# Attention and mixture-of-experts kernel: the maxima's split and the routing steps of five portions moved in the order of the work

## The reference

```python
# attention: 16 heads of 8, causal, keys and values from ctx (120 positions)
h = layernorm(x)
Q, K, V = h @ wq.T + bq, ctx @ wk.T + bk, ctx @ wv.T + bv
p = softmax(where(causal & not padded, Q K^T / sqrt(8), -inf))
x = x + (p V) @ wo.T + bo
# experts: 8, each token goes to its best 2; one shared expert for all
h = layernorm(x)
s = sigmoid(h @ gate_w + bias); top, idx = top_k(s, 2); w = top / (sum(top) + 1e-6)
o = 0.1 * (shared_mlp(h) + sum_k w_k * mlp[idx_k](h))       # mlp: 128 -> 512 -> gelu -> 128
x = x + o / (max|o| + 1e-6)
```

## Time and profile before

| | |
|---|---|
| profiled execution | 850.22 us, span 848.50 us |
| PE busy | 755.0 us (89%) |
| VectorE (DVE) busy | 646.8 us (76%) |
| ScalarE (ACT) busy | 636.9 us (75%) |
| GpSimd (POOL) busy | 539.9 us (64%) |
| mean granted TensorE clock | 0.968 |

### The profile page before, as it was taken

How to read it: one execution, slowest core, us unless ns; L and a number is a source line. 1 busy time by engine, 2 the same in 40 slices (tenths; PEclk the granted TensorE clock), 3 DMA queues, 4 the chain that set the end, 5 groups by cost and what they waited for, 6 DMA issues and landing times.

```text
span 848.5 us, 21662 instructions
## 1 busy us (share of the span) xinstructions
PE 755.0 (89%) x6977; PEld 512.5 (60%) x6977; DVE 646.8 (76%) x1774; ACT 636.9 (75%) x1185; POOL 539.9 (64%) x634
## 2 busy tenths in 40 slices
PE   5899899987998999988978869999999999979994
PEld 2345455544554555444445647788888888868773
DVE  5766778789688786876756796877778787767897
ACT  3589889877777787777579958888888888869630
POOL 6566666879777887777567773156656665654540
PEclk9999999999999999999898989999999999999998
DMA  4552544441222122211101144667767788782973
GB/s 127 178 192 63 187 137 125 139 146 58 75 66 74 58 86 66 75 60 58 36 8 48 60 160 145 227 236 262 259 236 248 273 296 278 269 279 88 276 232 100
DMA packets 100934, 126.97 MB, mean 150 GB/s; under 512 B 20919, under 2 KB 82039, under 8 KB 94807
## 3 DMA queue, kind: packets, MB, share of 16 engines
q1 hardware_dynamic: 92183, 107.08, 39.4%
q0 software_dynamic: 8640, 18.50, 6.2%
HBM read 77.84 MB, written 39.64 MB: 138 GB/s over the span
## 4 chain that ended last, share of the span: by engine, by line
PE 52%; POOL 13%; DVE 12%; issue 11%; ACT 9%; SPq 2%; DMA 1%; DVEq 0%; ACTq 0%; POOLq 0%
PE bank L1373 5%; PE bank L1385 4%; PE bank L1459 4%; PE bank L1460 4%; PE bank L1461 4%; PE bank L1448 4%; PE bank L1449 4%; PE bank L1450 4%; POOL xs_scratch L1227 4%; ACT prob L781 4%; POOL y_scratch L1234 3%; POOL prob L1212 3%; PE bank L1369 2%; PE bank L1353 2%; PE bank L1328 2%
## 5 line engine op out<-in xcount | busy, mean ns | idle before, releaser
L781 ACT ACTIVATE prob<-bank,padb,sc 120x512 f32<-120x512 f32 x256 | 178.1, 776 | 71.5 <-PE bank L1373 71.4
L1234 POOL DMA_INDIRECT y_scratch<-yo,ti x142 | 141.3, 995 | 121.3 <-DVE yo L1135 89.4
L1212 POOL TENSOR_SCALAR_AFFINE_SELECT prob<-prob 120x512 f32<-120x512 f32 x256 | 159.6, 634 | 81.4 <-ACT prob L781 76.1
L853 DVE TENSOR_REDUCE nm<-bank 128x4 f32<-128x480 f32 x256 | 150.3, 649 | 54.6 <-PE bank L1353 54.5
L1112 DVE TENSOR_TENSOR gl<-gf,gh 128x512 fp32r<-128x512 f32 (+1 forms) x220 | 143.2, 655 | 47.0 <-ACT gh L829 46.0
L1227 POOL DMA_INDIRECT xs_scratch<-x2r,idx x128 | 129.4, 1011 | 33.4 <-issue 32.7
L829 ACT ACTIVATE gh<-gf 128x512 fp32r<-128x512 f32 (+1 forms) x220 | 132.5, 602 | 5.1
L823 ACT ACTIVATE gf<-bank,wt 128x512 f32<-128x512 f32 (+1 forms) x156 | 99.8, 640 | 5.2 <-DVE gl L1112 4.7
L1373 PE MATMUL bank<-qblk,kT 32*120 32x512 f32 x512 | 74.8, 628 | 0.0
L1385 PE MATMUL bank<-prob,vm 120*32 120x128 f32 x2048 | 70.7, 280 | 2.7 <-ACT vm L750 1.6
L1353 PE MATMUL bank<-kblk,qT 32*128 32x480 f32 x512 | 71.9, 633 | 1.0 <-DMA kblk<-kT 1.0
(11 more groups left out here) (202 smaller groups left out, 1660.7 us busy)
## 6 DMA issues: line engine op xcount, KB each, us to landing
wt<-w_scratch SPq DMA_DIRECT2D x39, 1032.0 KB, 5.1
xt<-xs_scratch SPq DMA_DIRECT2D x32, 280.0 KB, 4.7
w_scratch<-x2t SPq DMA_DIRECT2D x8, 1024.0 KB
wt<-y_scratch SPq DMA_DIRECT2D x28, 256.0 KB, 4.9
xs_scratch<-padc SPq DMA_DIRECT2D x15, 280.0 KB, 2.8
x<-in_x SPq DMA_DIRECT2D x16, 256.0 KB, 3.2
qblk<-qT SPq DMA_DIRECT2D x64, 64.0 KB
x_scratch<-x SPq DMA_DIRECT2D x16, 256.0 KB, 2.4
```

What stands on the lines that cost most here:

```text
L781: e.activation(prob[u % NP][0:LK, :], banks[bi][0:LK, :], ACT.Exp, scale=sc[0:LK, 0:1], bias=padb[0:LK, t:t + 1]).then_inc(a_ex, 1)
L853: e.tensor_reduce(nm[:, g, i // 2, :], bk[:, 0:480].rearrange("p (j k) -> p j k", j=4), AX.X, ALU.max, negate=True).then_inc(v_mx, 1)
L1212: e.affine_select(out=pv, in_=pv, compare_op=ALU.is_ge, fill=0.0, base=0, pattern=[[0, 4], [1, 128]], channel_multiplier=-1).then_inc(p_cu ...
L1234: e.indirect_dma_start(y_dram, bass.IndirectOffsetOnAxis(ap=ti_[r % NWS][:, c:c + 1], axis=0), yo_[r % NYO][:, c, :], None).then_inc(d_y[r ...
```

## The change

It moves stages in the order. No instruction is added or removed.

```diff
         if n < NG - 1:
-            at(o + 3 + .43, "nm", n)
+            at(o + 3 + .20, "nm", n)
             at(o + 3 + .84, "nmT", n)
...
     for p, (a, z) in enumerate(PORTIONS):
         s = 7.0 * (4 * z + 10) - end
-        times = LATE_PORTION.get(p, (s + .8, s + 4.8, s + 11.8, s + 32.6, s + 32.8, s + 25.8, s + 38.9, 7.0))
+        times = LATE_PORTION.get(p, (s + .8, s + 25.8, s + 39.8, s + 47.0, s + 53.0, s + 53.4, s + 58.9, 7.0))
         for (stage, i), time in zip((("er", 0), ("route", 0), ("route", 1), ("rank", 0), ("place", 0), ("route", 2)), times):
```

## The result

Six runs of the changed kernel took 856.50 to 865.38 us, median 861.03; six of the kernel before, taken with them, had a median of 850.89. The ratio is 1.0116 (95% interval 1.0074 to 1.0158): the change makes the kernel slower, where 839 us was predicted. The profiled execution took 862.87 us, its span 861.1 (before 848.50); PE is busy 756.0 us, about as before (755.0).

A forecast was written before the change was run, and what follows sets the result against it. The first phase was taken as bound by a TensorE-ScalarE loop with 25.8 us of stalls. Terms summed to -12.2 us, 850.22 to 838.0 profiled, predicted median 839.0 us; range 833 to 845, over cases 829 to 849.

The forecast's parts named there:

- rank to kind 0, place to the next slot: First phase: rank keeps one of two banks, k waits for oT and tz starts 1.9 us later, five times; costs 9.5 us.
- nm behind the maxima: Six slots with scatters: nm no longer stands behind nb2, so nmT follows tO at once; gains 15.1 us.
- The portions' moves without the hold: Route 0's and the weights' collision gain of 10.7 us, less 1.5, 1.0 and 1.0 us for split, route 0, router.
- Route 0: Moved to kind 1, it frees its place in kind 2 and just fits the new one; costs 0.2 us five times.
- nmT's wait below 6 us: Sign of being right: nmT's wait for nm on TensorE falls from 18.8 us to under 6.
- PEld's wait for oT at k in exactly five slots: Sign of being right: k waits for oT in exactly five slots of kind 1, these some 2 us longer.
- place and route 2 ahead of router: In kind 1 on VectorE, router stands behind both and V waits for its bank; costs 0.2 us five times, 1.0 us.
- slots of kind 3 below 8 us: Sign of being right: no slot of kind 3 takes above 8 us with scatters running.
- 315 us for the twelve groups: Sign of being right: the twelve four-slot groups of the first phase take about 315 us instead of 326.62.
- rival 3: GpSimd's selects hold nm's second instruction at its new place, norm to oT wait; 20 us in five groups, 859 us; 9%.
- Rival 4: nm comes early, but nmTs, behind nb2 and route 1, is late for B; half of 15.1 us returns, 846.5 us; 6%.
- Rival 2, the clock: The bank's wait drops TensorE's clock, 1.7 us five times, 8.5 us more, 847.5 us; 17%.

The follow-up runs named there:

- run 9: Changed kernel with place directly behind rank, so rank's bank goes back at once but behind x2T's; ratio 1.0038 to the kernel before.
- run 10: As run 9, with rank and place together moved ahead of x2T, so PV gets a long-free bank; ratio 0.9822 to the kernel before.
- run 5: Changed kernel with rank behind PV and tO of the same slot, so only k and tz share a bank; 850.62 us.
- run 1: Changed kernel without the hold: rank directly in front of place, its bank given back at once; 839.67 us.
- run 2: Kernel before with only nm moved behind the last maxima; 841.15 us, ratio 0.9870.
- run 7: Run 1 with route 1 one slot on, in kind 0, where VectorE waits for a load anyway; 837.41 us.
- run 8: Run 7 with portion 5's route 0 also one slot on; 833.42 us, ratio 0.9791 to the kernel before.
- run 3: Changed kernel with nm back at its old place, so only the portions' steps and scatters are moved; 860.51 us.
- run 11: Run 1 with nm back at its old place, so neither nm's move nor the hold; 847.85 us, ratio 0.9944.

## Why the prediction was wrong

**The step that failed is "rank to kind 0, place to the next slot".** It said that with one bank "k waits for oT", tz for kT, 1.9 us five times. I listed PV among the stages that must take the other bank, and then priced only k and tz. PV comes first, and the other bank is the one that x2T has just filled, behind four exps on ScalarE. The changed kernel shows both, the PV hop 2.19 us and the tz hop 0.75. In the twelve groups PV's hop alone is worth 16.9 us (run 9 against 10), k's and tz's alone 9.1 (run 5 against 1), together 334.96 - 315.49 = 19.5. They don't add: where PV is late, ScalarE has emptied everything else, oT follows PV at once, and the k stretch is only 7.22 us against 6.71 where the clock is whole. It is whole in two of the five. In the others TensorE runs at 1.2 GHz for 3.4, 3.4 and 6.8 us from about PV's wait on, and the k stretches take 8.74, 7.75 and 9.10 us: 3.9 of the 19.5. The step held 9.5 us; 10.0 are missing.

**The terms of the gain were too large.** Without the bank the prediction has -22.3 us for the twelve groups (-15.1 - 10.7 + 1.5 + 1.0 + 1.0); run 1 has 315.49 - 326.62 = -11.1.

- "nm behind the maxima" at -15.1: alone it brings 317.26 - 326.62 = -9.4 (run 2). The wait goes, and the five slots priced at 11.6 give 12.6. But the sixth, priced at 3.5, gets 0.9 longer, since nmTs is late there (run 2), and the one at 173.00 grows by 1.6: I gave the neighbours nothing back.
- The portions' moves without the hold at -7.2: measured 315.49 - 317.26 = -1.8. Route 0 itself came out about as said: the two stretches at its old place take 359.14 - 346.15 = 12.99 us in the changed kernel (13.61 in run 1) where they took 8.72 + 6.34 (from 338.43, around), and the one at its new place is no longer than before, 6.64 us. But route 1, to which the prediction gives no cost, since it stays in a slot of kind 3, came to stand beside selects. That costs three stretches 0.9 us each, 2.7 of the missing 5.4 (run 7, 3.0 by run 8); the rest stays open.

These two, 11.2 us, the bank's 10.0, a start 1.1 us later and an end 2.5 us longer than priced make 24.8 of the 24.9 us between 838.0 and 862.87. The end, 861.1 - 437.95 = 423.15 us against 420.02, lay anywhere from 418.3 to 422.8 in runs 1, 3, 5, 7 and 8, which keep the scatters' move, so I can't say what of it is the late scatters.

**What was right.** Of the signs named: nmT's wait below 6 us, rs2 directly behind the selects, B not stopped beside route 0, PEld's wait for oT at k in exactly five slots, V not late. place and route 2 ahead of router show no cost: the stretch with V is 5.20 us, in the kernel before 5.19. Not so: slots of kind 3 below 8 us (the five with the wait take 9.84 to 11.71), the k stretches some 2 us longer (0.6 where the clock is whole, as PV takes most of it), and 315 us for the twelve groups.

**The rule weighed** (the Trainium skill, "SBUF — State Buffer", "Who interferes with whom": the one that contends is an instruction of VectorE with two SBUF inputs, beside a GpSimd instruction that reads SBUF). I tried it on the one instruction that the change moves, as rival 3, and stopped. That one was mostly safe: 0.23 or 0.24 us in nine of its eleven times between 102.99 and 437.95. The trace agrees with the rule for others that came beside selects: L966 2.64 us and 0.23 with none beside it, nm's second 2.90 at its old place (run 11). Each of the maxima, a reduction from PSUM, takes 0.64 to 0.66 us, beside selects too. How long such an instruction is held, the runs show differently from place to place (last section).

Rival 3 happened twice in the twelve groups. Ahead of the tO at 154.22 nm's second takes 1.23 us beside the weights' split and tO waits 0.84 us for norm; the stretch up to it is 6.52 us, 1.05 longer than before. Ahead of the tO at 186.86 the first takes 2.28; the stretch up to it and the next take 13.83 us, before 16.38. So it is about 1 us of the loss at most. Rival 4 shows in one slot of run 2. Rival 2, the clock, came with three of PV's five waits, as a follower of the bank's wait, not in place of it, and cost 3.9 us in the k stretches where 8.5 was priced.

## What to carry over

When a step keeps a buffer of a first-in, first-out pool longer, walk the pool through the order, name for each later taker which buffer it gets and who empties that last; here the first taker paid most, and a kernel with the same order and another turn of the pool (run 10) can be faster than either. When the order on GpSimd shifts, list which VectorE instruction now stands where each of its long runs begins, also those that the change doesn't touch. Price a removed stall by the group of slots and not by its own slot, for what comes next takes part of it back.

## What the runs showed of the hardware

A VectorE instruction with two inputs from SBUF that meets GpSimd's selects can be held for more than one of them (2.39 / 4 = 0.60 us each): 2.64 us over four, and 4.12 and 4.23 us where the weights' split stands in front and it ends with the third select. But it isn't always held to the end of the run. In the kernel before, GpSimd's four selects and what VectorE does beside them:

```profile
127.82 2.64 POOL L1212 TENSOR_SCALAR_AFFINE_SELECT prob<-prob 120x512 f32<-120x512 f32 x4 [3.32 <-ACT prob L781]
```

```profile
127.86 0.68 DVE L908 TENSOR_TENSOR nm<-nm 128x64 bf16<-128x64 f32 x1
...
128.69 0.50 DVE L964 TENSOR_TENSOR eq<-s,m 128x64 f32<-128x64 f32 x1
129.23 0.63 DVE L966 TENSOR_TENSOR eq<-eq,con 128x64 f32<-128x64 f32 x1
```

Here three get in, one after each of the first three selects. These start 0.66 us apart and those of the long holds 0.60, but nb2 of the earlier trace rows, beside selects 0.60 apart, was let in after two. What decides it is open. A conversion with one SBUF input was held too, 2.28 us against 0.21: L906 of the changed kernel, then GpSimd's selects:

```profile
182.90 2.28 DVE L906 CAST nm<-nm 128x64 bf16<-128x64 f32 x1
```

```profile
183.31 2.39 POOL L1212 TENSOR_SCALAR_AFFINE_SELECT prob<-prob 120x512 f32<-120x512 f32 x4
```

It ends at 185.18, with the third select (183.31 + 3 x 0.60 = 185.11).
